# A decoder layer whose feed forward computes gate, up and the first Hadamard stage with features on the partitions

## What is computed

```python
gate = bitlinear(x, w_gate)                 # act_quant(x) @ ternary(w).T, 512 -> 2048
up = bitlinear(x, w_up)                     # 512 -> 2048
intermediate = silu(gate) * up
return h_bitlinear(intermediate, w_down)    # act_quant(fwht(.)) @ ternary(w).T, 2048 -> 512
```

## Time and profile before

| | |
|---|---|
| median of 3 runs | 1714.65 us |
| the profiled execution, its time | 1715.27 us |
| its span, first to last instruction | 1713.4 us |
| TensorE busy | 1613.7 us (94%) |
| VectorE busy | 1063.9 us (62%) |
| ScalarE busy | 673.0 us (39%) |
| GpSimd busy | 396.7 us (23%) |
| mean granted clock of TensorE | 0.986 |

### The profile page before, as it was taken

One profiled execution on the slowest core, in us unless ns is written; L12 is line 12 of the kernel. 1 busy time (PEld: TensorE's weight loads), 2 busy tenths in 40 slices (PEclk: granted clock), 3 DMA queues, 4 the chain that ended last, 5 costly groups with the idle time before them and its releaser, 6 DMA issues.

```text
span 1713.4 us, 25662 instructions
## 1 busy us (share of the span) xinstructions
PE 1613.7 (94%) x10434; PEld 1300.0 (76%) x10434; DVE 1063.9 (62%) x1986; ACT 673.0 (39%) x1271; POOL 396.7 (23%) x270
## 2 busy tenths in 40 slices
PE   7999999999999999999999999998779999999996
PEld 5888887888887788888788887777558677676774
DVE  4555565555566565556656656657666777767665
ACT  4332333332333222333233233322255675756663
POOL 1111102001110203334333333420022322322220
PEclk9999999999999999999999999999889999999998
DMA  7111102011110101211121111204000000000000
GB/s 251 34 55 38 38 29 64 25 44 50 37 50 19 63 1 32 74 44 50 50 67 38 62 62 44 55 27 166 1 13 1 19 14 7 25 7 13 13 7 25
DMA packets 44293, 73.54 MB, mean 43 GB/s; under 512 B 3216, under 2 KB 24848, under 8 KB 43792
## 3 DMA queue, kind: packets, MB, share of 16 engines
q1 hardware_dynamic: 42256, 65.61, 12.2%
q0 software_dynamic: 1920, 6.29, 0.9%
HBM read 61.41 MB, written 10.49 MB: 42 GB/s over the span
## 4 chain that ended last, share of the span: by engine, by line
PE 63%; DVE 21%; issue 9%; POOL 3%; ACT 3%; DMA 0%; SPq 0%; DVEq 0%; POOLq 0%
PE bank L344 12%; PE bank L346 11%; PE bank L345 11%; PE bank L552 4%; DVE OG L976 4%; PE bank L453 3%; POOL sm L1258 3%; PE bank L598 2%; DVE sm L967 2%; DVE ZT L915 2%; DVE AM L923 2%; PE bank L567 2%; PE bank L439 2%; PE bank L415 2%; PE bank L410 2%
## 5 line engine op out<-in xcount | busy, mean ns | idle before, releaser
L344 PE MATMUL bank<-Wh,XTh 128*128 128x512 f32 x512 | 211.5, 413 | 0.0
L346 PE MATMUL bank<-Wh,XTl 128*128 128x512 f32 x512 | 200.8, 392 | 0.0
L345 PE MATMUL bank<-Wl,XTh 128*128 128x512 f32 x512 | 199.9, 390 | 0.0
L684 ACT ACTIVATE V<-bank 128x256 f32<-128x256 f32 x128 | 49.1, 384 | 373.9 <-PE bank L346 373.9
L1258 POOL TENSOR_TENSOR sm<-sm,half 128x8 f32<-128x8 f32 x32 | 52.8, 1649 | 523.0 <-DVE sm L970 523.0
L344 PE MATMUL bank<-XTh,Wh 128*128 128x512 f32 x384 | 161.0, 419 | 12.7 <-DVE XTl L865 12.7
L346 PE MATMUL bank<-XTh,Wl 128*128 128x512 f32 x384 | 151.2, 394 | 0.0
L345 PE MATMUL bank<-XTl,Wh 128*128 128x512 f32 x384 | 150.5, 392 | 0.0
L905 DVE SCALAR_TENSOR_TENSOR U<-U,bank 128x256 f32<-128x256 f32 x128 | 53.7, 419 | 149.1 <-ACT U L686 149.1
L552 PE MATMUL bank<-W,XT 128*128 128x512 bf16 x512 | 124.6, 388 | 13.2 <-ACT XT L771 13.2
L1289 POOL TENSOR_TENSOR HS<-HS,UB 128x512 f32<-128x512 f32 x64 | 89.7, 1402 | 197.2 <-DVE HS L1120 113.4
(11 more groups left out here) (188 smaller groups left out, 3454.3 us busy)
## 6 DMA issues: line engine op xcount, KB each, us to landing
RAW<-wgT SPq DMA_DIRECT2D x16, 512.0 KB, 3.8
RAW<-wuT SPq DMA_DIRECT2D x16, 512.0 KB, 3.7
RAW<-wdT SPq DMA_DIRECT2D x16, 512.0 KB, 3.7
w_scratch<-BW POOLq DMA_DIRECT2D x24, 256.0 KB, 4.4
W<-w_scratch SPq DMA_DIRECT2D x3, 2048.0 KB, 14.6
RAW<-Wo SPq DMA_DIRECT2D x8, 512.0 KB, 3.9
Y<-x SPq DMA_DIRECT2D x4, 1024.0 KB, 11.7
out<-Y SPq DMA_DIRECT2D x16, 256.0 KB, 2.0
```

The source lines that it names most:

```text
L344: engine.matmul(o, lh(c), rh(c), start=c == 0, stop=False)
L345: engine.matmul(o, lh(c), rl(c), start=False, stop=False)
L346: last = engine.matmul(o, ll(c), rh(c), start=False, stop=c == n - 1)
```

## The change

Gate and up are now made with features on the partitions: the weights are stationary, the 512 tokens of a whole batch move. An iteration n is a block j of 128 features of batch b, n = 16 b + j.
- The scale per token now runs along the columns. x_turned gets four small matmuls ("spread") which copy the scale to all partitions, and ScalarE puts it into SB.
- VectorE makes GS = gate * SB out of the bank, then M = up * GS. ScalarE takes tanh of GS in place, then adds 1 in place. GpSimd makes M = GS * M.
- The features already lie on the partitions, so turn1 falls away. M is split into a high part HI (ScalarE) and a rest LO (GpSimd), and had1 is two fp32r passes of 512 columns against the 128 matrix. The high and low parts of step n are ordered on ScalarE and GpSimd with gate of step n + 1.
- ScalarE copies the result into EV. SP writes it to a DRAM scratch and, when a batch is complete, reads it back tile by tile into Z, regrouped so that had2 finds its 128 rows of 8 times 16 features on the partitions. turn2 falls away. The columns of w_down are permuted on the host to match, and the 16 matrix becomes blocks of 16.
- had1 comes three iterations behind gate, had2 22, read of tile i at n = 4i + 18, quantise 4i + 26, clamp 4i + 27, turn_q 4i + 28, down 4i + 29, store 4i + 30; 91 iterations. ctx and qk of batch 1 move ahead of gate 0, the other cross stages two iterations earlier. XT is doubled, QK now shares ATh's memory.
- The scales of the quantisation are arranged anew; one VectorE operation with two SBUF inputs falls away from the chain, and two of the one-column operations at x_round.

```diff
-    for n in range(64 + 17):
-        if 0 <= n - 6 < 64:
-            yield "turn2", n - 6
-        if 0 <= n - 7 < 64:
-            yield "had2", n - 7
+    yield CROSS[0], 1
+    yield CROSS[1], 1
+    for n in range(64 + 27):
+        if 0 <= n - 22 < 64:
+            yield "had2", n - 22
         if n < 64:
             yield "gate", n
-        if 0 <= n - 2 < 64:
-            yield "had1", n - 2
-        if 0 <= n - 1 < 64:
-            yield "turn1", n - 1
...
+        if 0 <= n - 3 < 64:
+            yield "had1", n - 3
+        if n % 4 == 2 and 0 <= (n - 18) // 4 < 16:
+            yield "read", (n - 18) // 4
+        if n % 4 == 3 and 0 <= (n - 27) // 4 < 16:
+            yield "clamp", (n - 27) // 4
+        if n % 4 == 2 and 0 <= (n - 26) // 4 < 16:
+            yield "quantise", (n - 26) // 4
+        if n < 46:
+            yield CROSS[(n + 2) % 16], (n + 2) // 16 + 1
...
# TensorE
+                    bk = take(("spread", b), (S["s_evac"], b + 1))
+                    pe.wait_ge(S["x_scaled"], b + 1)
+                    for i in range(4):
+                        mm = engine.matmul(bk[:, 128 * i:128 * i + 128],
+                                           ax[:, b, 2, i:i + 1].broadcast_to([128, 128]), IDN, start=True, stop=True)
...
-                            mm = engine.matmul(bk[:], XT[:, c, 128 * (i % 4):128 * (i % 4) + 128],
-                                               w[:, c, 512 * q:512 * q + 512], start=c == 0, stop=c == 3)
+                            mm = engine.matmul(bk[:], w[:, c, 128 * j:128 * j + 128], XT[:, b % 2, c, :],
+                                               start=c == 0, stop=c == 3)
...
                 elif stage == "had1":
                     bh = take(("h1", n), (S["h1_evac"], n + 1))
+                    pe.wait_ge(S["h_hi"], n + 1)
+                    engine.matmul(bh[:], H128[:], HI[:, n % 2, :], start=True, stop=False)
+                    pe.wait_ge(S["h_lo"], n + 1)
+                    engine.matmul(bh[:], H128[:], LO[:, n % 2, :], start=False, stop=True).then_inc(S["had1"], 1)
+                elif stage == "had2":
+                    pe.wait_ge(S[f"z_in{i % 2}"], 16 * (i // 2) + 16)
                     for c in range(4):
+                        mm = engine.matmul(bh[:, 128 * c:128 * c + 128], Z[:, i % 2, 4 * q + c, :], C[:, 4, :],
+                                           start=True, stop=True)
# ScalarE
+            def high(n):
+                act.wait_ge(S["h_made"], n + 1)
+                act.wait_ge(S["had1"], n - 1)
+                engine.activation(HI[:, n % 2, :], M[:, n % 3, :], ACT.Copy).then_inc(S["h_hi"], 1)
...
                 if stage == "gate":
+                    if n:
+                        high(n - 1)
+                    act.wait_ge(S["m_made"], n + 1)
+                    engine.activation(GS[:, n % 2, :], GS[:, n % 2, :], ACT.Tanh).then_inc(S["h_tanh"], 1)
+                    act.wait_ge(S["h_tanh"], 2 * n + 1)
+                    engine.activation(GS[:, n % 2, :], GS[:, n % 2, :], ACT.Identity,
+                                      bias=ONE[:, 0:1]).then_inc(S["h_tanh"], 1)
                 elif stage == "had1":
+                    act.wait_ge(S["had1"], n + 1)
+                    act.wait_ge(S[f"z_out{n % 2}"], 16 * (n // 2))
+                    engine.activation(EV[:, n % 2, :], bank("h1", n)[:], ACT.Copy).then_inc(S["h1_evac"], 1)
# VectorE
                 if stage == "gate":
+                    dve.wait_ge(S["gate"], n + 1)
+                    dve.wait_ge(S["s_evac"], b + 1)
+                    dve.wait_ge(S["h_made"], n - 1)
+                    engine.tensor_tensor(GS[:, k, :], bank("gate", n)[:], SB[:, b % 2, :], ALU.mult).then_inc(S["gs_made"], 1)
+                    dve.wait_ge(S["up"], n + 1)
+                    dve.wait_ge(S["gs_made"], n + 1)
+                    dve.wait_ge(S["h_lo"], n - 2)
+                    engine.tensor_tensor(M[:, n % 3, :], bank("up", n)[:], GS[:, k, :], ALU.mult).then_inc(S["m_made"], 1)
# GpSimd
+            def low(n):
+                pool.wait_ge(S["h_hi"], n + 1)
+                pool.wait_ge(S["had1"], n - 1)
+                engine.tensor_tensor(LO[:, n % 2, :], M[:, n % 3, :], HI[:, n % 2, :], ALU.subtract).then_inc(S["h_lo"], 1)
...
                 if stage == "gate":
+                    m = M[:, n % 3, :]
+                    pool.wait_ge(S["h_tanh"], 2 * n + 2)
+                    engine.tensor_tensor(m, GS[:, n % 2, :], m, ALU.mult).then_inc(S["h_made"], 1)
+                    if n:
+                        low(n - 1)
# SyncE
+                elif stage == "had1":
+                    b, j = divmod(n, 16)
+                    sp.wait_ge(S["h1_evac"], n + 1)
+                    engine.dma_start(zs[b].rearrange("a (r j) t -> (a r) j t", j=16)[:, j:j + 1, :],
+                                     EV[:, n % 2:n % 2 + 1, :]).then_inc(S[f"z_out{n % 2}"], 16)
+                elif stage == "read":
+                    b, i = divmod(n, 4)
+                    for k in range(2):
+                        sp.wait_ge(S[f"z_out{k}"], 16 * 8 * (b + 1))
+                    sp.wait_ge(S["had2"], 4 * n - 4)
+                    engine.dma_start(Z[:, n % 2], zs[b].rearrange("a q t -> q a t")[:, :, 128 * i:128 * i + 128]
+                                     ).then_inc(S[f"z_in{n % 2}"], 16)
```

More of the change, by code:

```diff
@@ L85, in ffn_order @@
 def ffn_order():
-    for n in range(64 + 17):
-        if 0 <= n - 6 < 64:
-            yield "turn2", n - 6
-        if 0 <= n - 7 < 64:
-            yield "had2", n - 7
+    yield CROSS[0], 1
[3 more added lines that the diff above has]
+            yield "had2", n - 22
         if n < 64:
             yield "gate", n
-        if 0 <= n - 2 < 64:
-            yield "had1", n - 2
-        if 0 <= n - 1 < 64:
-            yield "turn1", n - 1
[L98 to L111, removed]
+        if 0 <= n - 3 < 64:
[8 more added lines that the diff above has]
+            yield CROSS[(n + 2) % 16], (n + 2) // 16 + 1
+        if n % 4 == 0 and 0 <= (n - 28) // 4 < 16:
+            yield "turn_q", (n - 28) // 4
+        if n % 4 == 1 and 0 <= (n - 29) // 4 < 16:
+            yield "down", (n - 29) // 4
+        if n % 4 == 2 and 0 <= (n - 30) // 4 < 16:
+            yield "store", (n - 30) // 4
 def raw_tasks():
@@ L149 @@
 x1_turned x1_hi x1_lo xm xm_add n1_stats n1_aggr n1_var n1_rstd n1_applied n2_stats n2_aggr n2_var n2_rstd n2_applied
-x_absmax x_limit x_scale x_scales x_scaled x_round xq_made xq_turned xt_evac idb_made
-gate up gate_tanh gate_act up_evac h_made h_turned sp_s had h1_evac h1_turned sp_v had2 h2_evac h_absmax h_scale f_made
+x_absmax x_limit x_scale x_scaled x_round xq_made xq_turned xt_evac x_spread s_evac idb_made
+gate up gs_made m_made h_tanh h_made h_hi h_lo had1 h1_evac z_out0 z_out1 z_in0 z_in1 had2 h2_evac h_absmax h_scale f_made
 h_round hq_made hq_turned hq_evac0 hq_evac1 down ffn_add n3_stats n3_aggr n3_var n3_rstd n3_applied
@@ L562, in ffn @@
                 elif stage == "had1":
                     bh = take(("h1", n), (S["h1_evac"], n + 1))
-                    pe.wait_ge(S["sp_s"], n + 1)
-                    for c in range(4):
[L566 to L581, removed]
+                    pe.wait_ge(S["idb_made"], 2)
@@ L764, in cross @@
                         engine.activation(XI[:, i, :], Y[:, 4 * b + i, :], ACT.Identity,
[L765 removed]
+                                          scale=ax[:, b, 1, i:i + 1], bias=half[:, 16:17]).then_inc(S["x_round"], 1)
                 elif stage == "x_turned":
@@ L778, in cross @@
                     engine.activation(IDB[:], IDN, ACT.Copy).then_inc(S["idb_made"], 1)
+                    engine.activation(H128[:], C[:, 3, :], ACT.Copy).then_inc(S["idb_made"], 1)
+            def high(n):
+                act.wait_ge(S["h_made"], n + 1)
+                act.wait_ge(S["had1"], n - 1)
+                engine.activation(HI[:, n % 2, :], M[:, n % 3, :], ACT.Copy).then_inc(S["h_hi"], 1)
             def ffn(stage, n):
-                i, q = divmod(n, 4)
                 if stage == "gate":
[L783 to L795, removed]
-                elif stage == "had1":
[L797 to L801, removed]
@@ L1115, in ffn @@
             def ffn(stage, n):
[L1116 removed]
                 if stage == "gate":
[L1118 to L1125 removed]
+                    b, k = n // 16, n % 2
+                    dve.wait_ge(S["gate"], n + 1)
[6 more added lines that the diff above has]
+                    engine.tensor_tensor(M[:, n % 3, :], bank("up", n)[:], GS[:, k, :], ALU.mult).then_inc(S["m_made"], 1)
                 elif stage == "had2":
+                    i, q = divmod(n, 4)
                     dve.wait_ge(S["h2_evac"], n + 1)
```

112 lines of the change are left out of this document (52 added, 60 removed).

## The result

The changed kernel takes 1764.39 us (median of 4 runs, 1763.98 to 1765.01) against 1714.63 (now 4 runs of the kernel before, 1714.58 to 1715.28): a ratio of 1.029, 95% interval 1.0272 to 1.0307. It is slower, by 49.8 us; forecast were 1751 and a range of 1700 to 1788. The profiled execution took 1764.3 us; its span is 1762.5 us (1713.4 before), the mean granted clock 0.958 (0.986).

A forecast was written before the change was run, and what follows sets the result against it. A wait cycle between ScalarE and VectorE, 21.8 us a round, was to replace TensorE's 21.9 as the bound. Stretches 1264 + 114.6 + 169 + 98 + 104 made 1749.6, with profile offsets 1751 us; range 1700 to 1788.

The forecast's parts named there:

- The ring: Closed wait cycle of ScalarE and VectorE (H2, reduction, GS, M, tanh, +1, EV): 4.49 us per iteration, 21.8 per round.
- TensorE still binds the body: Rival for the gates: ScalarE and VectorE run far enough apart, TensorE sets the pace, 1657 us; chance 0.10.
- TensorE's gain: Feed forward: transposes and fp32 had1 go, two fp32r passes (0.55 us) come; 1.2 us saved per iteration, 78 over 64.
- Head: Before the gates: ctx and qk of batch 1 come first, so gate 0 starts at 1264 instead of 1255.5.
- Gates 0 to 21: First stretch, cross attention but no H2: sixteen iterations 82.9, six more 28.0, 3.7 for energies awaiting qk: 114.6 us.
- Gates 22 to 45: Middle stretch: cross stages 38.2 and 82.9, H2 with its reduction 19, five rounds of tile work 29: 169 us.
- Gates 46 to 63: Last stretch of gates, after cross attention: 18 iterations at 5.45 us, 98 us.
- low clock in the body: Part of the worse rival: with port meetings and late reads, 0.5 us more per iteration, 2 per tile, 1800; chance 0.10.
- Tail: After the last gate: six tiles one behind the other, closes 15.6 us apart, the last 13.4: 104 us.
- DMA: Scratch transfers: writes 2.0 us each, reads between 2.0 and 11.7, hidden; batch 3's ctx load held up 2 to 8.
- 4 in the sum: Allowance, in us, said to be counted for the read that holds up the ctx load of batch 3.
- The port: VectorE operations held by GpSimd's on the shared SBUF port: nothing charged, 0 to 8 us kept for the range.

The follow-up runs named there:

- opening it: Changed kernel with VectorE's reduction of H2 moved behind GS and M of the same iteration, gates 22 to 63: 1740.27 us.
- loading it: Changed kernel plus an unread 512-wide ScalarE copy per gate 22 to 63: between +1 and EV 1780.16 us; ahead of tanh's wait for M 1763.57.

## Why the prediction was right, and where it was off

- *The ring.* Right, and the core of the forecast. The iteration with only the clamp beside the ring takes 4.48 us (GS of gate 55 to that of 56), 4.49 was forecast; HT adds 0.92 (0.95 forecast), the wait for down 0.55 (0.55), quantise 2.26 (2.33, where its rows show 2.28). That makes 21.65 us for a round against 21.8, shown by opening it (24.1 us less) and by loading it (15.8 more, or nothing beside it). The rival "TensorE still binds the body" (1657) is out for this kernel, and is what happens in the rounds once the ring is open and quantise is early (17.02; 17.1 was forecast for TensorE alone). The condition that the text gave for it, a ring below 4.26 us, left out the 3.8 us of tile work per round; by the text's own sum the ring would have had to be below 3.3. One sign missed: TensorE was busy for 87% of the quiet round and 81% of the gates 46 to 63, not 75 to 80%, since 17.1 us of work had become 18.9 at the lower clock.
- *TensorE's gain.* The step was sized a little high: had1 took 0.66 us from its first pass (1603.85) to the next stage (1604.51), 0.55 was forecast. Without effect, as TensorE had slack.
- *Head.* Gate 0 at 1264.43, forecast 1264, in part by luck: the load was issued at 1250.1, 1.8 us earlier than the row used, but landed after 5.4 instead of 4.1, and the twelve passes took 5.3 instead of 4.5. The first GS came 3.6 us after gate 0 (1268.07), behind the second qk's evacuation and two norm statistics on VectorE. The forecast has this wait of gate 0 for qk, but in the next stretch, as "3.7 more at the first".
- *Gates 0 to 21.* 118.5 against 114.6, and against 110.9 without those 3.7 us, which had passed before the first GS, so this part was 7.6 too low. 6.2 of it are the two iterations with ctx and qk, 22.9 us from the GS of gate 14 to that of 16 (3.5 and 19.4), where 16.7 was forecast (7.8 and 8.9). The 8.9 had TensorE's twelve passes at 2.8, their length at full clock; they took 5.2 (1348.17 to 1353.36), since the engine had idled 9.96 us. The prediction charged this restart in the head and forgot it here.
- *Gates 22 to 45.* 174.1 against 169. Same step (23.8 us for ctx and qk), and the context load behind the read: 5.50 us of waiting where 4.1 was put. The 169 itself is less sure than it looks: it counts a round of tile work at 5.8 us, where the ring's sum has 3.8, and doesn't say why.
- *Gates 46 to 63.* 95.0 us for the 17 intervals, 5.6 for a gate, scaled to 18 gates 100.5, against 98. Rounds took 21.65 but for one of 23.24: in it down took 5.21 us (1619.62) instead of 3.61 (1597.97), after TensorE had idled 2.31, and had2 and H2 came late by it. The forecast had this in a rival ("low clock in the body") and not in the sum. Elsewhere the lower clock cost nothing, as with had2 at 1592.53, 2.02 us instead of 1.05 in a round of 21.66. The rest of the 2.5 us comes from the scaling, since the 17 intervals hold five of the long ones and the eighteenth would be a short one.
- *Tail.* 101 against 104, closes 14.2 to 15.9 us apart against 15.6. Right, and for the reason given: moving quantise ahead of the close took 25.8 us off what follows the last GS, 29.8 in all. That it would be so cheap to mend, the text did not see.
- *DMA.* The writes took 2.0 us as forecast, the reads 5.8, between the bounds, and TensorE waited 0.5 us in all for Z. The load behind the read landed 6.9 us after its issue (1440.72), the one of batch 2, with no read before it, after 4.1: held up by 2.8, within the 2 to 8. The "4 in the sum" stand in none of the terms that make the 169.
- *The port.* Nothing was charged, 0 to 8 kept. On the lines view from 1200 on, the norm at L1009 rose from 540 ns to 753 (32 times) and the one at L1176 from 540 to 653 (16 times), 8.6 us more, and the two operations on four columns (L1104, L1106) by 4.0 in all; but the clamp fell from 992 to 685 (32 times), 9.8 us less, the scaling of XI (L1014, now L1017) from 653 to 543 (16 times), and XQ (L1112) from 1090 to 685 (8 times), 5.0 less. The sum is near nothing, counted in VectorE's busy time, not on the path.

The misses add up: 0.4 + 3.6 + 3.9 + 5.1 + 2.5 - 2.7 = 12.8 of the 12.9 us by which the span is longer than forecast; with the 3.7 us put where they passed, the first two are 0.4 and -0.1, and the gates 0 to 21 carry 7.6.

## What to carry to other kernels

When work is taken off the engine that binds, follow one iteration round all engines and add up the cycle of waits before counting the gain: here the cycle was as long as TensorE's round before the change, and one reduction written two places later gave 24 us. Where a change makes the pipeline longer, look at what is left for the end and whether the first step of a tile needs anything of the tile before; if only the written order says so, change the order. What is late has a successor, as GpSimd's low half behind the context load, so ask for the next one before pricing a repair. And leaving an operation out also leaves out the waits that its engine made for it, so look at what else moved.

## What was not expected of the hardware

- *The port holds the smallest operations too.* Timelines of DVE and POOL of the changed kernel, an operation on four columns beside GpSimd's:
```profile
1544.34 1.10 DVE L1104 TENSOR_SCALAR ax<-ax,ws 128x4 f32<-128x4 f32 x1
1545.35 0.22 DVE L1106 TENSOR_SCALAR ax<-ax,ws 128x4 f32<-128x4 f32 x1
```
```profile
1544.15 1.27 POOL L1286 TENSOR_TENSOR LO<-M,HI 128x512 fp32r<-128x512 f32 x1
```
The first took 1.10 and ended with GpSimd's operation (1545.44 and 1545.42); at 1246.17, with GpSimd idle, it took 0.20. The prediction's rows showed this only with two inputs in SBUF, while the Trainium skill ("SBUF — State Buffer", Who interferes with whom) names `tensor_scalar` as well; here the trace agrees with it.
- *Restarts.* Over the changed kernel and its variants the first qk pass took 0.79 or 0.80 us after TensorE had idled 4.33 to 13.7 us, and 0.50 after 1.6 to 4.1. In the tail of the changed kernel down took 3.62 and 4.50 to 4.59 in turn and 6.20 at the end, at a granted clock of 0.80 over the stretch.
